# Score sums ahead of the experts' second layer, unread products around the experts, another order of the dispatch, and first expert rows loaded by two engines

## The reference

```python
# second layer's attention: 16 heads of 8, window of 7 tokens
attn = jnp.einsum('bhld,bhlkd->bhlk', q, kg) + bias[None]
attn = jax.nn.softmax(attn, axis=-1)
out = jnp.einsum('bhlk,bhlkd->bhld', attn, vg)
...
# second mixture: two entries of a router over the mean token, mixed into weights of 6 experts
expert_weights = jnp.einsum('bk,bke->be', topk_vals, pw[topk_idx])
h = jax.nn.gelu(jnp.einsum('bsd,edf->ebsf', x, W1) + b1[:, None, None, :], approximate=False)
out_e = jnp.einsum('ebsf,efd->ebsd', h, W2) + b2[:, None, None, :]
return jnp.einsum('be,ebsd->bsd', expert_weights, out_e)
```

## Time and profile before

| | us |
|---|---|
| median of 3 runs | 850.82 |
| lowest and highest | 850.41, 851.25 |
| profiled execution | 852.73 |
| its span, first to last instruction | 850.9 |
| PE busy | 627.5 (74%) |
| DVE busy | 631.8 (74%) |
| ACT busy | 523.5 (62%) |
| POOL busy | 283.8 (33%) |
| mean granted clock | 0.868 |

### The profile page before, as it was taken

The page is one execution under the profiler, slowest core; times in us unless marked ns, Lnnn a source line. Parts: engine busy times, 40 slices in busy tenths (PEclk is TensorE's granted clock), DMA queues, the critical chain, the costliest instruction groups (busy, mean ns, idle before and its releaser), DMA issues.

```text
span 850.9 us, 10931 instructions
## 1 busy us (share of the span) xinstructions
PE 627.5 (74%) x3132; PEld 481.1 (57%) x3133; DVE 631.8 (74%) x1271; ACT 523.5 (62%) x837; POOL 283.8 (33%) x313
## 2 busy tenths in 40 slices
PE   6998543461835628297863799787999999999897
PEld 4554543461835628274543799534766766766665
DVE  1786698999999999997874122267888888887753
ACT  1588999999989999942322234244457456564542
POOL 0465000000000000001576244315656666664632
PEclk9999875876958778599685799967999999999999
DMA  5380044444555444525102466200000000000000
GB/s 176 118 296 24 1 83 71 84 71 84 97 101 107 75 83 71 89 53 185 49 27 65 132 172 172 60 27 1 1 1 9 2 10 10 1 10 9 1 10 18
DMA packets 26379, 56.50 MB, mean 66 GB/s; under 512 B 4199, under 2 KB 15568, under 8 KB 25856
## 3 DMA queue, kind: packets, MB, share of 16 engines
q0 software_dynamic: 5728, 24.56, 15.4%
q1 hardware_dynamic: 20032, 30.90, 12.1%
q10 hardware_dynamic: 576, 0.52, 0.2%
HBM read 29.91 MB, written 10.17 MB: 47 GB/s over the span
## 4 chain that ended last, share of the span: by engine, by line
PE 41%; DVE 22%; issue 14%; ACT 12%; DMA 4%; POOL 3%; POOLq 1%; SPq 1%; DVEq 0%; ACTq 0%; another core or an unknown queue 0%
PE psum L2023 6%; PE psum L1741 3%; DVE s_R L1259 3%; DVE s_R L1246 3%; DVE s_R L1270 3%; PE psum L2010 3%; PE psum L1942 2%; PE psum L2056 2%; PE psum L1950 2%; PE psum L2011 2%; PE psum L2012 2%; DVE s_R L1251 2%; PE psum L1813 2%; PE psum L2079 2%; PE psum L1814 1%
## 5 line engine op out<-in xcount | busy, mean ns | idle before, releaser
L1813 PE MATMUL psum<-s_xn_lo,s_split_hi 128*128 128x368 f32 x256 | 94.0, 367 | 137.7 <-ACT s_R L908 134.7
L1813 PEld LDWEIGHTS psum<-s_xn_lo,s_split_hi 128*128 128x128 f32 x256 | 54.3, 212 | 142.2 <-ACT s_R L908 137.4
L668 POOL DMA_DIRECT2D s_xnfm<-s_R x14 | 17.1, 1219 | 255.8 <-DVE s_R L1270 255.8
L1265 DVE TENSOR_TENSOR_SCAN s_R<-s_R 128x2944 f32<-128x2944 f32 x16 | 100.7, 6292 | 0.8
L2023 PE MATMUL psum<-s_R 128*128 128x368 f32 x256 | 89.8, 476 | 2.5 <-DVE s_R L1538 2.5
L1814 PE MATMUL psum<-s_xn_hi,s_split_lo 128*128 128x368 f32 x256 | 91.3, 357 | 0.0
L1815 PE MATMUL psum<-s_xn_hi,s_split_hi 128*128 128x368 f32 x256 | 91.0, 356 | 0.0
L1041 ACT ACTIVATE s_R<-psum,s_cols 128x368 f32<-128x368 f32 x96 | 49.4, 565 | 65.7 <-PE psum L2012 65.6
L727 POOL TENSOR_TENSOR s_R<-s_R 128x368 f32<-128x368 f32 x47 | 54.5, 1159 | 61.4 <-DVE s_R L1538 38.2
L764 POOL TENSOR_TENSOR s_R<-s_R 128x368 f32<-128x368 f32 x48 | 46.6, 971 | 53.1 <-DVE s_R L1668 51.4
L915 ACT ACTIVATE s_R<-psum,s_cols 128x736 f32<-128x736 f32 x64 | 55.8, 875 | 12.4 <-PE psum L1815 8.0
(11 more groups left out here) (254 smaller groups left out, 1639.9 us busy)
## 6 DMA issues: line engine op xcount, KB each, us to landing
s_xnfm<-s_R POOLq DMA_DIRECT2D x14, 1472.0 KB, 10.5
s_R<-in_w SPq DMA_DIRECT2D x28, 256.0 KB
s_R<-in_xg SPq DMA_DIRECT2D x7, 744.0 KB, 4.3
x_sorted<-in_x_init SPq DMA_DIRECT2D x1, 5082.0 KB
s_wBC<-in_wBC SPq DMA_DIRECT2D x8, 256.0 KB, 2.7
s_R<-in_v SPq DMA_DIRECT2D x2, 1024.0 KB
s_R<-x_sorted SPq DMA_DIRECT2D x28, 66.0 KB
s_R<-in_w SPq DMA_DIRECT2D x1, 1536.0 KB, 6.7
```

The lines of the kernel that those rows point to most:

```text
L1265: dve.tensor_tensor_scan(bufB[:, u], ra[:, u], bufB[:, u], 0.0, ALU.mult, ALU.add).then_inc(ra_free, 1)
L1813: pe.matmul(bank(c), w_hi[:, s, u, k, :], xn_lo[:, a:b], start=True, stop=False)
```

## The change

It has five parts. PE's score sums go ahead of tiles 18 and 19, and tiles 20, 21 go behind the transposed scores; tiles 28 to 31 are spread over earlier places of the step, and the router's product goes ahead of tiles 8 to 11. DVE weighs expert 5 ahead of the first offset instead of behind it, and in the last two steps the rest after experts 0 and 1. The unread products become fewer in the dispatch's first three groups and in the attention's pause, and more in three places around the experts, one of them new. POOL computes a reciprocal deviation after one scatter instead of two. The first chunk of expert rows is loaded in halves, by SP and ACT.

```diff
@@ SP: the first chunk of OG
-                sp.dma_start(seqs(OG, c), y_rows[c * CT:(c + 1) * CT].rearrange("(b l) d -> l b d", l=L))\
+                n = 2 * L if c == 0 else CT
+                sp.dma_start(OG[:, c * CB:c * CB + n // L, :],
+                             y_rows[c * CT:c * CT + n].rearrange("(b l) d -> l b d", l=L))\
                     .then_inc(og_ready[c % 2], 16)
@@ POOL: dispatch
-                    scatter(i, 0, 2)
+                    scatter(i, 0, 1)
                     rstd_c(2 * i + 3)
-                    scatter(i, 2, BP)
+                    scatter(i, 1, BP)
@@ ACT: end of the experts
+            for s in range(NSL):
+                act.wait_ge(ot_stored[s], 16 * (NTILE // NSL))
+            act.dma_start(OG[:, 2:CB, :], y_rows[2 * L:CT].rearrange("(b l) d -> l b d", l=L)).then_inc(og_rest, 16)
             stage_end(act, 4)
@@ DVE: first_experts
+                    if j == 2:
+                        dve.wait_ge(og_rest, 16)
@@ DVE: step of the last stage
                     expert_weights(f - 1)
-                    if not att:
-                        weigh_rest(f - 1)
                 weigh_expert(f - 1, 0)
                 weigh_expert(f - 1, 1)
+                if 0 <= f - 1 and not att:
+                    weigh_rest(f - 1)
...
                     shares_rest(c)
+                weigh_expert(f - 1, 5)
...
                             stream_sums(f)
-                        weigh_expert(f - 1, 5)
@@ PE: dispatch, experts
-                    keep_busy_3(2)
+                    keep_busy_3(1)
...
-                    keep_busy_3(4)
+                    keep_busy_3(5)
...
+            def keep_busy_4(n):
+                for _ in range(n):
+                    pe.matmul(bank(5), ident[:, :], w2[:, 0].rearrange("p j d -> p (j d)")[:, 0:CT], start=True,
+                              stop=True)
+
+            keep_busy_4(11)
+            pe.wait_ge(scat_done, 16 * B)
+            keep_busy_4(2)
...
             pe.wait_ge(og_ready[0], 16)
-            keep_busy(6)
+            keep_busy(9)
@@ PE: step of the last stage
-                ffn(f - 1, 18, 19)
                 result_tm(c - 3)
-                ffn(f - 1, 19, 20)
                 if att:
                     scores(c)
-                ffn(f - 1, 20, 22)
+                ffn(f - 1, 18, 20)
                 if att:
                     scores_tm(c)
+                ffn(f - 1, 20, 22)
...
-                        fill_pause(3)
+                        fill_pause(1)
...
                     elif 1 <= o <= 3:
+                        if o == 1:
+                            ffn(f - 1, 28, 30)
                         ffn(f, 2 * o - 2, 2 * o)
                     elif o == 4:
-                        ffn(f - 1, 28, 30)
+                        ffn(f - 1, 30, NF)
                     elif o == 5:
-                        ffn(f - 1, 30, NF)
                         ffn(f, 6, 8)
                     elif o == 6:
-                        ffn(f, 8, 10)
                         if tail:
                             router_spread(f)
-                        ffn(f, 10, 12)
+                        ffn(f, 8, 12)
```

More of the change, by code:

```diff
@@ L413, in audio_tower @@
         og_ready = [sem("og_ready0"), sem("og_ready1")]
+        og_rest = sem("og_rest")
         d_end = taken[0]
```

## The result

| | before | after |
|---|---|---|
| median, us | 850.95 (4 runs) | 839.83 (4 runs) |
| lowest and highest | 850.41, 851.25 | 838.13, 841.30 |
| ratio, 95% interval | | 0.9867 [0.9849, 0.9884] |
| profiled execution, span | 852.73, 850.9 | 838.13, 836.3 |

The kernel became 11 us faster, not 24. The two traces side by side show where. The last two columns are the difference at each landmark and the difference that the terms of the prediction add up to there.

What follows compares the result with a forecast made beforehand. No engine alone was taken as the bound; a full step was bound by PE except for a wait on DVE's and ACT's softmax. Terms 11.4 + 4.3 + 3.4 + 0.8 + 1.8 + 2.6 = 24.3 us gave 827 us, range 820 to 837.

Steps and rivals of the forecast that it cites:

- Experts' start: Start of the experts: unread products run while scatters land, so the first tile meets a high clock; 3.4 us gained.
- Full steps: Last stage, c = 2 to 7: earlier softmax and no wait for the low part; 1.9 us a step, 11.4 us in six.
- The score sums' part: Each full step: score sums ahead of two second-layer tiles start the softmax earlier; 1.1 us a step.
- the low part's wait: Each full step: PE's wait behind the second spread product is filled by tiles 28 and 29; 0.8 us a step.
- Dispatch: Dispatch: fewer scatters and unread products ahead of DVE's work remove POOL's idle time before later groups; 4.3 us gained.
- First step of the last stage: After the experts: nine instead of six unread products keep the clock high for the first query and key products; 1.8 us.
- Rows by two engines: First chunk of expert rows: two queues move the halves at once, so DVE starts earlier; 0.8 us gained.
- Last two steps: Last two steps: experts 0 and 1 weighed first, so PE's waits for their bank go; 2.6 us, bounds 1.5 and 3.0.
- DVE did not become the bound: Rival for full steps: DVE becomes the bound, only the 0.8 us a step is gained; 833 us; chance 0.17.
- the clock stayed at 1.0: Rival, slower: PE's clock falls in the full steps' pause before the shares, costing 30 us; 856 us; chance 0.03.
- The gains around the experts don't come: Rival: dispatch, experts' start, row loading and first last-stage step reach only their lower bounds; 834 us; chance 0.13.

Runs made afterwards that it cites:

- the control: The changed kernel itself, unedited, timed again in the third session beside the versions that combine edits: 839.31 us, 0.9855 of the kernel before.
- the run on chip C without the filling: Fastest version with two instead of three unread products behind the experts' stage wait and none behind the first two transposes: 832.1 us, 0.9766 of before.

## Why the prediction was wrong

The predicted 827 us missed the measured 839.8 us, and so did the range of 820 to 837. The direction was right. Step by step:

- *Experts' start: this step failed.* "The new products run from DVE's last instruction of the routing" is not so: PE waits for the end of the stage first, and that includes POOL's last scatter. So the products began after the rows' issue and not 9 us ahead of it. Instead of -3.4 us the stage from issue to issue takes 74.47 - 70.93 = +3.5 us, an error of 6.9 us, more than half of the gap between 24.3 and 14.6 us. The runs show it: without the products 4.4 us faster than the control, and with the products alone 6.5 us slower than before. Where I had assumed them they are no better than none (0.9805 against 0.9803); only with the pauses filled too do they gain 3.4 us, the 3.4 of the prediction. Line 181's wait could not be seen in the earlier trace rows: PE's 15.51 us were put down to the rows, which came last, and the earlier gate stood hidden behind them. It stood in the code, though, right ahead of the insertion.
- *Full steps: mechanism right, size 1.6 instead of 1.9 us.* The score sums' part came as worked out, and so did the low part's wait. The router's product waits 0.42 us where I had "0.1 us at most"; put back, a step is 2.1 us shorter than before. The account closes: a step lost 1.35 us of unread products, and PE's idle time in it went from 2.14 to 1.90 us, together 1.6. At c = 1, where I had counted nothing, the same product waits 1.08 us. So the term of 11.4 us measured 6 x 1.6 - 1.1 = 8.5 us.
- *Dispatch: right in that trace, wrong as a size.* I took all of POOL's idle time in the earlier trace rows as the kernel's own, and DVE's 1.38 us as a wait for PE's counts, which had ended 1.0 us before. Like for like the gain is 2.0 us, and none where DVE stalls. That the first pair of traces showed 3.6 of the 4.3 us is luck.
- *First step of the last stage: total right, cause in doubt.* The stretch from the load's issue to the first shares is 3.1 us shorter where 2.6 us were forecast for it and the row loading. That is partly luck: the two traces on chip A stand 26.27 - 24.71 = 1.6 us apart. And from DVE's first chunk to these shares it is 21.4 to 23.1 us in four traces of the old order with six products, 21.2 us in two of the new order with six, and 20.6 us with nine: how long the clock holds there differs from run to run by more than the three products bring, and I had put all of it down to them.
- *Rows by two engines: 0.5 us instead of 0.8.* Two queues moved 72 to 87 GB/s together from 542 to 545 us, the pace of the one; the second half came 0.35 us behind. This is the rule that I had weighed and set aside: in the Trainium skill, "DMA: Bandwidth & Descriptors", section "Issuing engines are not separate DMA queues", a second issuer saves only issue time. My reading of the 0.29 busy share against it was wrong; the trace agrees with the rule as far as the rate goes, and what was gained is that DVE could begin on the first half.
- *Last two steps: 3.5 us instead of 2.6.* From the shares of c = 7 to the end it is 57.0 instead of 61.1 us. Of the 4.0 us 0.5 stand ahead of the next step's project products (19.97 instead of 20.49 us behind the shares); the other 3.5 are the last two steps', 0.5 us above my upper bound. No wait above 0.33 us is left there, and the waits for the banks account for 2.5 of the 3.5.
- *The errors add up.* Experts' start 6.9, full steps 2.9, dispatch 0.7; in the other direction rows and first step 0.5, last two steps 0.9; and 0.5 us lost from c = 0 to c = 1: 9.6 of the 9.7 us between 24.3 and 14.6.
- *Rivals.* DVE did not become the bound, and the clock stayed at 1.0 from 600 to 835 us with a pause of 0.89 us and one unread product in each step. "The gains around the experts don't come" was nearest in place, but its lower bound of +1.5 us was itself too high: nothing in it allowed the products to cost time. I had bounded a loss only by a late clock, not by the products' own 10 us.

## What to carry to other kernels

Before unread work is put into a pause, list every wait ahead of it on its engine, not only the one that the trace names: where two gates stand in a row, a trace shows the later one, and work behind both is on the path. Bound such an insertion from below by its whole duration. And compare two executions of the unchanged kernel before idle time in one of them is counted as a gain.

## What was not expected of the hardware

- DVE waits that no engine, DMA or semaphore in the profile ends ("remote"), nearly always at the same instructions, those that take PE's counts, 0.9 to 5.7 us long. The products that DVE takes have ended long before: in the run with the dispatch alone 2.6 and 4.2 us. In the dispatch they stand in all seven traces of chips B and C, in none of the eight of chip A, and in the one of the kernel before that the prediction used. With them the new dispatch takes 50.0 us from first to last scatter, without them 46.7. The two DMA queues that the profile names instruction queues move the same bytes with such waits and without (0.33 to 0.34 and 0.19 MB), which neither points to the loading of instructions nor rules it out. What DVE waits for stays open.
- Eight products of 128 x 128 x 128 take 2.05 us at the low clock and 1.06 to 1.13 us at the high one, in all runs alike. 26 unread records ahead of them took 10.15 to 10.9 us, the clock rising on the way; where the first tile came at the low clock, the fourth first layer stood 11.0 to 12.2 us behind the rows' issue, and at best 9.2 us. The whole worth of an early high clock at this place is 2 to 3 us, and 10 us of unread work on the path can't earn it.
- The clock, once high, fell within 10 us in one trace with four pauses of 0.5 to 1 us at the start of the stage, and stayed high for 99 us in another with two of them filled. Pauses of this length don't bring it down every time: it stayed high over two of 0.55 us in the changed kernel, and over 0.68 and 0.55 us in the run on chip C without the filling.
